# Two attention layers on one core: another order for the prologue, with other clears, selection rows and products of zeros

## The reference, cut to what matters

```python
x1 = layer_norm(x, ln1_w, ln1_b)                    # x: (4, 256, 256)
q = x1 @ q_w + q_b                                  # 16 heads of 16
k, v = ctx @ k_w + k_b, ctx @ v_w + v_b             # ctx: (4, 512, 256)
scores = where(mask, q @ k.T / 4, smallest)
hidden = softmax(scores) @ v @ cproj_w + cproj_b + x
y = gelu(layer_norm(hidden, ln2_w, ln2_b) @ fc_w + fc_b) @ proj_w + proj_b
h = hidden + y
out = h + alpha * softmax((h @ w_q.T) @ (ctx @ w_k.T).T / 16) @ (ctx @ w_v.T) @ w_o.T
```

## Time and profile before

| what | value |
|---|---|
| median of 3 runs | 310.41 us (308.37 to 323.36) |
| the profiled execution's own time | 313.87 us |
| its span, first to last instruction | 312.1 us |
| busy: PE, DVE, ACT, POOL | 86%, 68%, 57%, 29% of the span |
| chain that ended last, by engine | PE 54%, DVE 13%, DMA 8%, ACT 8%, POOL 7% |
| mean granted clock of TensorE | 0.973 |

### The profile page before, as it was taken

The page is one execution under the profiler, slowest core; times in us unless marked ns, Lnnn a source line. Parts: engine busy times, 40 slices in busy tenths (PEclk is TensorE's granted clock), DMA queues, the critical chain, the costliest instruction groups (busy, mean ns, idle before and its releaser), DMA issues.

```text
span 312.1 us, 5297 instructions
## 1 busy us (share of the span) xinstructions
PE 268.1 (86%) x2012; PEld 214.4 (69%) x2012; DVE 212.4 (68%) x368; ACT 176.6 (57%) x329; POOL 89.3 (29%) x108
## 2 busy tenths in 40 slices
PE   0757878997998699898988799998999999898995
PEld 0644647794676588676876587775877798578974
DVE  6776685677589458965488498847478766366854
ACT  3221575668472485956371786765375777526622
POOL 5551011102022139530012257430031174344100
PEclk9989599999799799999999999999999999999999
DMA  6038847711359002111638030205055000000000
GB/s 211 1 97 159 225 90 224 188 54 27 79 135 207 13 28 51 46 34 58 130 104 175 2 75 4 79 0 110 11 192 81 3 0 2 0 0 2 2 34 34
DMA packets 16456, 23.16 MB, mean 74 GB/s; under 512 B 2528, under 2 KB 9184, under 8 KB 16416
## 3 DMA queue, kind: packets, MB, share of 16 engines
q1 hardware_dynamic: 13360, 17.31, 23.8%
q10 hardware_dynamic: 3072, 5.52, 6.4%
HBM read 12.07 MB, written 1.05 MB: 42 GB/s over the span
## 4 chain that ended last, share of the span: by engine, by line
PE 54%; DVE 13%; DMA 8%; ACT 8%; POOL 7%; issue 5%; SPq 3%; ACTq 0%; POOLq 0%; DVEq 0%
PE work_ps L621 11%; DMA k_stack<-kp_l 8%; PE s L672 7%; PE om L703 6%; PE s L693 6%; PE work_ps L625 5%; DVE neg_max L1411 5%; PE work_ps L608 4%; ACT probs L1107 2%; PE s L621 2%; PE om L679 2%; SPq L520 2%; POOL ft L1771 2%; POOL max_cols L1727 1%; DVE ft L1480 1%
## 5 line engine op out<-in xcount | busy, mean ns | idle before, releaser
L1411 DVE TENSOR_REDUCE neg_max<-s 128x1 f32<-128x512 f32 x128 | 83.7, 684 | 20.8 <-PE s L672 20.3
L1107 ACT ACTIVATE probs<-s 128x512 f32<-128x512 f32 x128 | 75.5, 599 | 29.2 <-PE s L693 28.7
L693 PE MATMUL s<-q_stack,k_stack 128*128 128x256 f32 x256 | 57.5, 308 | 6.2 <-ACT probs L1107 5.4
L672 PE MATMUL s<-k_stack,q_stack 96*128 96x512 f32 x128 | 53.8, 453 | 4.7 <-DVE neg_max L1411 4.2
L693 PEld LDWEIGHTS s<-q_stack,k_stack 128*128 128x128 f32 x256 | 44.6, 200 | 14.0 <-ACT probs L1107 8.0
L672 PEld LDWEIGHTS s<-k_stack,q_stack 96*128 96x128 f32 x128 | 24.0, 202 | 20.9 <-DVE neg_max L1411 12.5
L703 PE MATMUL om<-probs,vals 128*17 128x256 f32 x512 | 33.7, 382 | 0.0
L1727 POOL CAST max_cols<-neg_max 128x8 fp32r<-128x8 f32 x16 | 5.8, 363 | 96.3 <-DVE neg_max L1411 96.3
L1099 ACT ACTIVATE q_stack<-om 8x1024 fp32r<-8x1024 f32 x16 | 16.3, 1018 | 8.1 <-PE om L679 7.8
L703 PEld LDWEIGHTS om<-probs,vals 128*17 128x17 f32 x512 | 11.9, 96 | 10.7 <-issue 0.3
L1422 DVE TENSOR_TENSOR y_l<-work_ps,y_h 128x512 fp32r<-128x512 f32 x12 | 8.3, 690 | 13.2 <-ACT y_h L1121 13.2
(11 more groups left out here) (290 smaller groups left out, 670.4 us busy)
## 6 DMA issues: line engine op xcount, KB each, us to landing
k_stack<-kp_h SPq DMA_DIRECT2D x32, 128.0 KB
cx<-in_ctx_t_dram SPq DMA_DIRECT2D x4, 512.0 KB, 4.5
k_stack<-kp_l SPq DMA_DIRECT2D x16, 128.0 KB
q_stack<-qp_h SPq DMA_DIRECT2D x32, 64.0 KB
pcx<-in_ctx_dram ACTq DMA_DIRECT2D x3, 512.0 KB, 4.7
pT_raw<-in_ctx_t_dram ACTq DMA_DIRECT2D x3, 512.0 KB, 9.8
xz<-in_x_dram SPq DMA_DIRECT2D x5, 256.0 KB, 4.1
q_stack<-qp_l SPq DMA_DIRECT2D x16, 64.0 KB
```

What stands on the lines that cost most here:

```text
L672: pe.matmul(s1[:, s1_bank(b, SLOTS * g + s), :], q_stack[0:ROW_MAX, hd, chunk(t)], k_stack[0:ROW_MAX, hd, :], start=True, stop=True).then_ ...
L693: mm = pe.matmul(s2[:, s2_bank(b, SLOTS * g + s), i * LQ:(i + 1) * LQ], k_stack[:, hd, chunk(k)], q_stack[:, hd, :], start=True, stop=True)
L1107: act.activation(probs[:, g % 2, s // 2, k:k + 2, :], s2[:, s2_bank(b, SLOTS * g + s), :].rearrange("p (k n) -> p k n", k=2), ACT.Exp).the ...
L1411: dve.tensor_reduce(neg_max[:, g % 2, s % 2, s // 2:s // 2 + 1], s1[:, s1_bank(b, SLOTS * g + s), :], AX.X, ALU.max, negate=True).then_inc ...
```

## The change

The prologue is rearranged; the iterations are as they were. The clears of group 1's stacks go from POOL to the head of DVE's prologue, those of group 2 behind POOL's second low keys. POOL's low part of wk waits for `z1_done`. The selection rows of all three groups are written by ACT, one activation of 32 partitions by 2048 columns each (`select`), in place of DVE's cast and of SP's two copies. The query bias goes ahead of the first keys on PE and DVE, and ACT's wv_h ahead of its first high keys. Group 0's three query DMAs are issued by ACT. SP issues group 1's stacks only when group 0's have landed, and group 2's ahead of the next mask and x. PE starts with 14 products of zeros; one more product whose result nobody reads follows each of the first eight `max_tile`; and the first two `max_tile` of group 1 go ahead of `max_rows(0, 0)`.

```diff
@@ SP prologue
-                sp.wait_ge(ones_done, 2)
-                sp.wait_ge(sel_done, 3)
+                sp.wait_ge(cleared[0], 2)
                 stack_keys(0, 0)
-                stack_queries(0, 0)
+                sp.wait_ge(cleared[1], 2)
+                sp.wait_ge(stacked[0], 16 * STACK_DMAS)
+                stack_keys(0, 1)
+                stack_queries(0, 1)
                 sp.wait_ge(ct_done, DC)
                 sp.dma_start(cx[:], ctx_t[1].rearrange("(c p) n -> p c n", p=P)).then_inc(cx_in, 16)
-                sp.wait_ge(gaps_done, STACK_GROUPS - 1)
-                stack_keys(0, 1)
-                stack_queries(0, 1)
-                for n in range(1, STACK_GROUPS):
-                    sp.dma_start(words(k_stack[ROW_MAX:ROWS, slots_of(0, n), :]), words(k_stack[ROW_MAX:ROWS, slots_of(0, 0), :])).then_inc(sel_in, 16)
+                sp.wait_ge(cleared[2], 2)
+                stack_keys(0, 2)
+                stack_queries(0, 2)
                 ...
-                stack_keys(0, 2)
-                stack_queries(0, 2)
@@ PE
+            def keep_busy(n):
+                for _ in range(n):
+                    pe.matmul(s2[:, 1, :], k_stack[:, GH, 0:P], k_stack[:, GH, :], start=True, stop=True)
             def prologue():
+                pe.wait_ge(cleared[1], 1)
+                keep_busy(14)
                 pe.wait_ge(consts, 1)
                 pre(0, U_ZT)
-                pe.wait_ge(wk_hi, 1)
-                pre(0, U_K)
                 ...
+                pe.wait_ge(wk_hi, 1)
+                pre(0, U_K)
                 ...
                 for s in range(SLOTS):
                     max_tile(0, 0, s)
+                    for _ in range(1):
+                        pe.matmul(s2[:, 1, :], wk[0][:, 0, 0:P], wk[0][:].rearrange("p c n -> p (c n)"), start=True, stop=True)
+                for s in MAX_TILES[0]:
+                    max_tile(0, 1, s)
                 max_rows(0, 0)
                 for s in range(START):
-                    attend(0, 0, s, 0)
+                    if s > 0:
+                        attend(0, 0, s, 0)
                     attend(0, 0, s, 1)
@@ ACT
+            def select(n):
+                act.wait_ge(sel_done, 2)
+                act.wait_ge(cleared[n], 2)
+                act.activation(k_stack[ROW_MAX:P, slots_of(0, n), :],
+                               sel_small[ROW_MAX:P, :].unsqueeze(2).to_broadcast([P - ROW_MAX, GH, LK]), ACT.Copy).then_inc(sel_rows, 1)
                 pre(0, U_ZT)
+                act.wait_ge(wv_in, 16)
+                act.activation(wv[0][:], raw_v, ACT.Copy).then_inc(w_hi, 1)
+                select(0)
                 key_high(0, 0)
                 act.wait_ge(bq_done, 2)
                 pre(0, U_Q)
-                act.wait_ge(wv_in, 16)
-                act.activation(wv[0][:], raw_v, ACT.Copy).then_inc(w_hi, 1)
+                for part, (made, n) in enumerate(((qh_done, 1), (pre_free, pre_use(0, U_Q)))):
+                    act.wait_ge(made, n)
+                    for i in [i for i, p in enumerate(TERMS_Q) if p == part]:
+                        act.dma_start(words(q_stack[term_rows(i), slots_of(0, 0), :]), words(qp[part][rows_of(0), 0, :])).then_inc(stacked[0], 16)
                 key_high(0, 1)
                 pre(0, U_V)
                 pre(0, U_V + 1)
+                select(1)
+                select(2)
                 max_rows(0, 0)
@@ DVE prologue
-                dve.wait_ge(sel_done, 2)
-                dve.tensor_copy(k_stack[ROW_MASK:P, slots_of(0, 0), :],
-                                sel_small[ROW_MASK:P, :].unsqueeze(2).to_broadcast([P - ROW_MASK, GH, LK])).then_inc(sel_done, 1)
+                dve.memset(words(k_stack[:, slots_of(0, 1), :]), 0.0).then_inc(cleared[1], 1)
+                dve.memset(words(q_stack[:, slots_of(0, 1), :]), 1.0).then_inc(cleared[1], 1)
                 ...
-                pre(0, U_K)
                 ...
+                pre(0, U_K)
                 key_low(0, 0)
@@ POOL prologue
-                pool.memset(words(k_stack[0:ROW_MASK, slots_of(0, 0), :]), 0.0).then_inc(ones_done, 1)
-                pool.memset(words(q_stack[:, slots_of(0, 0), :]), 1.0).then_inc(ones_done, 1)
+                pool.memset(words(k_stack[:, slots_of(0, 0), :]), 0.0).then_inc(cleared[0], 1)
+                pool.memset(words(q_stack[:, slots_of(0, 0), :]), 1.0).then_inc(cleared[0], 1)
                 rstd(ln1, ln1_step, 0, rstd1)
                 pool.wait_ge(wk_hi, 1)
+                pool.wait_ge(z1_done, 1)
                 pool.tensor_tensor(wk[1][:], raw_k, words(wk[0][:]), ALU.subtract).then_inc(wk_lo, 1)
                 mask_row_of(0)
-                for n in range(1, STACK_GROUPS):
-                    pool.memset(words(q_stack[:, slots_of(0, n), :]), 1.0)
-                    pool.memset(words(k_stack[:, slots_of(0, n), :]), 0.0).then_inc(gaps_done, 1)
                 key_low(0, 1)
+                pool.memset(words(k_stack[:, slots_of(0, 2), :]), 0.0).then_inc(cleared[2], 1)
+                pool.memset(words(q_stack[:, slots_of(0, 2), :]), 1.0).then_inc(cleared[2], 1)
```

More of the change, by code:

```diff
@@ L266, in build @@
         tail_y, tail_y_hi, tail_y_lo = sem("tail_y"), sem("tail_y_hi"), sem("tail_y_lo")
-        sel_in = sem("sel_in")
         pool_step = sem("pool_step")
@@ L270, in build @@
         dve_const = sem("dve_const")
-        lnq_done, gaps_done, ones_done = sem("lnq_done"), sem("gaps_done"), sem("ones_done")
+        lnq_done, sel_rows = sem("lnq_done"), sem("sel_rows")
+        cleared = [sem(f"cleared{g}") for g in range(STACK_GROUPS)]
         bq_ps, bq_done, prep_ps, prep_done = sem("bq_ps"), sem("bq_done"), sem("prep_ps"), sem("prep_done")
@@ L662, in max_tile @@
                     if b == 0 and g < STACK_GROUPS:
[L663 to L666, removed]
+                        pe.wait_ge(cleared[g], 2)
                 n = NS * b + SLOTS * g + s
@@ L685, in exp_tile @@
                 if b == s == 0 and g < STACK_GROUPS:
[L686 to L689, removed]
+                    pe.wait_ge(sel_rows, g + 1)
                 await_(pe, s2_free, s2_before(b, SLOTS * g + s))
```

## The result

| | before | after |
|---|---|---|
| median of the runs | 313.05 us (308.37 to 323.36, 4 runs) | 314.42 us (312.83 to 314.89, 4 runs) |
| profiled execution, its span | 313.87, 312.1 | 312.83, 311.1 |
| mean granted clock of it | 0.973 | 0.951 |

The two lie on either side of 1, both within 2%: no change that can be told. The forecast was 303.4, range 299.5 to 308.5. The ratios leave out runs more than 1.5% above the fastest of the same kernel, in the second measurement six of the changed kernel's twelve.

The account below looks back on a forecast made before the run. Bound: the first 33.3 us, a chain of latencies with no engine full. Next x's statistics at 31.8 instead of 38.80 win 7.0, taking 313.87 to 306.9; the median lies 3.5 below the profile, so 303.4; range 299.5 to 308.5.

Parts of the forecast that it names:

- the head: Prologue up to the values on PE: they start at 15.7, 5.25 earlier than 20.96, and last 2.9.
- Statistics: Norm statistics on DVE in the prologue start at 3.7 instead of 5.69.
- collision: POOL's wk part (1.26) fully blocks DVE's low parts, so z's low part starts at 10.6, not 9.3.
- bias: Query bias, 128 by 2, no longer held by POOL's clears: 3.5 of the 5.25 gained before the values.
- the 0.3 named as a sign: Sign that the forecast holds: the 128 by 2 bias operation takes below 0.3 us.
- The clears don't exclude each other: Clears on DVE and POOL run side by side at no cost; the opposite bound was POOL's 2.74 in full.
- Rival (a): No collision of POOL's wk part with DVE: values 1.3 earlier, total 302.1; chance 0.15.
- Rival (b): PE's clock stays low: values lose 1.6, first keys and queries 2.6, half hidden; total 306.3; chance 0.20.
- Nothing else is under way here, so I take 2.6: Stack landing after its last issue takes 2.6: group 0 landed at 17.6, group 1 at 24.2.
- rival (d): SP's wait counts slow landings twice; at 9.08 each, total 315.2; decides from a landing of 6.6; chance 0.05.
- 7.0 goes through the loop: Next x's statistics at 31.8 instead of 38.80; this 7.0 lead lasts through the loop to the end.
- Rival (c): The loop takes the lead back, as a load or stack in it doesn't come earlier: 310.4; chance 0.12.

Follow-up runs that it names:

- no_zeros: Changed kernel without the 14 products of zeros on PE; 313.64 us, 0.9931 against the kernel before.
- half_stack: Changed kernel with half of each row left out in group 0's key and query stack copies; 305.36 us (one run; before beside it 310.77).
- no_group_wait: Changed kernel with SP's wait for group 0's stack taken out; 312.05 us, 0.9942 against the kernel before.
- after_gaps: Changed kernel, SP's wait kept, plus 33 products of 256 columns in PE's waits of the first and second element; 309.37 us, 0.9941 against before.
- no_wait_gaps_only: Changed kernel without SP's wait, plus 33 products of 256 columns in PE's loop waits, no prologue fillers; 306.77 us, 0.9858 against before.
- spread_bias: Changed kernel with the loop's key preparation, including one-column bias products, moved to other slots; 311.73 us, 0.9995 against the kernel before.
- fill_all: Changed kernel plus 7, 8 and 5 products in prologue waits and 56 ahead of exponential products; 312.51 us, 1.0077 against the kernel before.
- before_again: The kernel before, unedited, run and profiled a second time; 310.81 us, 1.0049.
- before_gaps: Kernel before plus 33 products of 256 columns at the same places of the first and second element; 314.21 us, 1.0131 against before.
- no_wait_gaps: Changed kernel without SP's wait, with 7 and 5 prologue fillers and 33 products in PE's loop waits; 304.93 us, 0.9834 against before.
- no_wait_fill: Changed kernel without SP's wait, plus 7 and 5 filler products in the prologue; 309.16 us, 0.9958 against the kernel before.
- after_again: The changed kernel, unedited, measured a second time in 12 runs; 312.00 us, 0.9965 against the kernel before.
- fill_prologue: Changed kernel plus 7, 8 and 5 products in PE's prologue waits, none in the loop; 314.09 us, 1.0138 against the kernel before.

## Why the prediction was wrong, step by step

**Right: the head.** Statistics, collision and bias came within 0.5 each (the bias operation itself took 0.63 and not the 0.3 named as a sign), and the values started at 15.69 for 15.7, lasting 2.96 for 2.9. The clears don't exclude each other, as assumed (1.76 and 1.80 side by side). The collision of POOL's wk part with DVE's low parts is there (2.19 against 1.26); the Trainium skill's rule on it (SBUF — State Buffer, "Who interferes with whom") agrees with this trace. Rival (a) falls: in `no_zeros` z's high part is done at 9.09, and its low part still starts at 10.16, right behind wq's. Rival (b) falls for the head: the values ran at the upper clock. The zeros raised it for the transposes, the first keys and the queries, but the values ran at it without them too, in `no_zeros` and in the second trace of the kernel before.

**Wrong, first: "Nothing else is under way here, so I take 2.6"** for a stack's landing. It measured 4.73 and 3.57. The row of x gives the price of one load; a stack is six copies into 16 partitions each, some 590 KB together (three sets of 16 rows by 8 KB of keys and by 4 KB of queries), that stand in line behind one another. `half_stack` shows that the bytes set it. Through SP's wait it counts twice: the first exponential product missed by 3.24 (29.84 for 26.6), and the two landings were late by 2.63 (20.23 for 17.6) and, beyond that, 0.9 (27.73 for 24.2 is 3.53); the maxima between, slowed by the fall of the clock at 22.02, hid behind the second. The statistics missed by 3.85 (35.65 for 31.8), and both things that they wait for were late: DVE's maxima of group 1 end at 35.62 (30.9 forecast), and x, issued behind the stacks at 31.09 (27.8), took 4.5 (4.0). This is the mechanism of rival (d), at a third of its size: a landing of 4.73 is a third of the way from 2.6 to its 9.08, short of the 6.6 from which the wait would have made the kernel slower by itself. What that wait is worth depends on the clock behind it: 0.34 at the first exponential product and 1.49 at the statistics in `no_group_wait`, where both stacks share the DMA engines, and 2.03 at the statistics between `after_gaps` and `no_wait_gaps_only`.

**Wrong, second: "7.0 goes through the loop".** At 35.65 the lead was 3.15, at 98.66 it was −3.57. The steps of the sum had no term for TensorE's clock behind the prologue, although showed a stretch at 0.50 there. PE waits there for stacks and ACT (1.52, 1.54 and 1.11 in the rows above), and its granted clock falls to the lower level, at 22.02, 28.84 and 39.08, and again at 69.80 and 80.04. From windows of 0.25 us, the time at the lower level between the second and the third element's high part of z, beside the time between these two (the code of the kernel before, but for what `gap` and `spread_bias` add or shift; `fill_all`, with 6.8 and 53.85, is left out, as its products lie on PE's path):

| traces | at the lower level | z to z |
|---|---|---|
| `no_wait_gaps_only` | 0 | 48.02 |
| before; `before_again`; `half_stack`; `spread_bias`; `after_gaps`; `before_gaps`; `no_wait_gaps` | 3.4 | 48.95 to 49.59 |
| `no_wait_fill` | 6.8 | 50.91 |
| after; `after_again`; `no_zeros`; `no_group_wait`; `fill_prologue` | 13.7 to 14.3 | 53.09 to 53.39 |

(Kernels with `gap` have 14 products more in that stretch, put into waits.) The time goes with the clock and not with the prologue: `after_gaps` has the changed kernel's prologue and takes 49.59, as the kernel before does (48.99 and 49.52). Between the second row and the last, some 10.6 more at the lower clock cost 3.9 (53.28 against 49.38 in the mean), or 0.37 for each. The Trainium skill (TensorE: Matmul & The Clock Gate, "HAM oscillation — how this bites in real kernels") prices such time at half, which would make 5.3; the traces show less, perhaps because part of it lies beside work of other engines, which no run here separates.

**Wrong, third: the 7.0 is a lead over one execution, taken off the median of others.** The profiled execution took 313.87 and the median run 310.41. In the second trace of the kernel before (309.74) the statistics come at 37.19, so the forecast's 31.8 is only 5.39 ahead. Most of the 1.61 between is the values' lower clock (1.40 at the first maximum), which the sum counted as won by the change.

**Rival (c): not shown.** Between the third and the fourth element the changed kernel seems to gain back 2.69 (66.49 against 69.18, with the wait of 9.08 in the latter). But the second trace of the kernel before takes 66.21 there and that of the changed kernel 66.54: the 2.7 belong to the first trace alone. And in `no_wait_gaps` a lead of some 5.2 goes through the loop, so that step of the prediction holds as long as the clock does. Put together, over the second trace: 7.0 forecast, less 1.61 for the trace it was read from, less 3.85 up to the statistics, less 0.72 up to the second element's high part of z, less 3.88 in the next element, makes a loss of 3.06 at the third high part of z, and it is 3.1 at the end.

**What stays open.** Why a stretch at the lower clock at 38 to 46 that lasts 6.8 is followed by two more at 68 to 87 (in all five traces of the last row) and a shorter or earlier one is not. The one experiment aimed at it, `spread_bias`, did not settle it. Nor is it settled what the change is worth at an equal clock: runs at 0.971 to 0.973 that enter the ratios took 308.89 (4 of the changed kernel) against 310.70 (24 of before, from all measurements) in the mean, some 1.8 us, which fits `after_gaps` but rests on few runs. With SP's wait out and the clock held up it comes out near the forecast (304.93 in `no_wait_gaps`, for 303.4).

## What to carry to other kernels

Price a stacking copy by its bytes through the DMA engines and not by the nearest single load, and count it twice where a wait puts the next one behind it. Read each step that is to be won from two traces of the unchanged kernel: here 1.61 us of the forecast and the longest wait of the loop belonged to one execution. When a change shortens a stretch in which PE is not the bound, look at what PE's waits do to its clock later on: a sum of latencies that leaves out the clock of an unchanged loop can miss by more than the whole gain. And compare runs with their granted clock beside the time, since a lead of 2 us can't be seen between runs whose clocks differ by 0.02.

## What was unexpected of the hardware

With seven, three and nine filler products of 256 columns in waits of PE (from 36.10, 37.95 and 39.80, `after_gaps`) the clock did not fall again until 69.04, where the changed kernel had it at the lower level from 39.08 to 45.91; 56 of them in busy places, with those of the prologue, raised it as well (0.984 over the run of `fill_all`) and gained nothing. Two clears on DVE and POOL, 1 MB each (1.76 and 1.80 us), don't slow each other.
